# Cross-attention on one core: pairs of batches with a shared tail chunk, chunks in groups of two, and a rolled TensorE loop

## The chip, the cores and the metric

The kernel runs on one core of a Trainium2 chip. Its time is the device time of one execution in microseconds (us). Three runs of the kernel before took 1699.2, 1699.8 and 1699.86 us; the median is 1699.8 us. The engines are TensorE (PE, with its weight loads listed as PEld), VectorE (DVE), ScalarE (ACT), GpSimd (POOL) and SyncE (SP), which issues DMAs.

## What is computed

The model is one layer: cross-attention of 16 batches of 64 queries to 1601 context rows each, causal self-attention, and a mixture of experts. The change touches the cross-attention, cut here to what matters:

```python
# x (16, 64, 512), y (16, 1601, 256); 16 heads of 32; y_dca = last 16 rows, y_main = the other 1585
q  = _ln((x @ Wq + bq).reshape(b, s1, H, HD), qn_w, qn_b)          # per head
kv = concatenate([y_main @ Wk + bk, y_main @ Wv + bv], -1).reshape(b, s2, H, 2 * HD)
k  = _ln(kv[..., :HD], kn_w, kn_b);  v = kv[..., HD:]
ctx     = _attn(qT, kT, vT)                                        # softmax over 1585 keys
ctx_dca = _attn(qT, k_dcaT, v_dcaT)                                # softmax over the 16 others
x = x + (ctx + ctx_dca) @ Wo + bo
```

## The kernel before

`prepare` makes the queries, the split weights and the keys and values of the 16 other rows. `cross_attention` walks over the 16 batches, and within a batch over 13 chunks (CH = 13) of 128 context rows; the last one (LAST = 12) holds 49 rows of the main context, and beside them the 16 other rows from partition 64 on. Then come `self_attention` and `experts`.

For one chunk the work is this. ScalarE rounds the context chunk to a high part (`y_high`, L851) and GpSimd subtracts it for the low part (`y_low`, L941). TensorE multiplies by the weights of the keys (`keys`, 6 matmuls of 512 columns) and of the values (`values`, 6 more), all recorded at L96 with the tiles wk and wv. VectorE adds the bias to the keys and so empties their PSUM bank (`k_bias`, L985), GpSimd squares them (`square`, L948), VectorE reduces per head (`k_reduce`, L991), ScalarE makes a seed for the inverse root (`seed`, L102 and L104), VectorE refines and applies it (`k_norm`, L109 to L113 and L1000). ScalarE empties the values' bank (`v_evac`, L870, or L868 for the last chunk). TensorE turns the normed keys with 4 transposes (`turn`, L77 on kn) and ScalarE copies them out (`k_evac`, L858). TensorE multiplies keys by queries (`scores`, L1104: weights of 64 rows by 128 columns), ScalarE takes exponentials (`exps`, L883), and TensorE sums the values (`weighted`, L1120: weights of 128 rows by 64 columns; for the last chunk twice, once for the main context and once for the other rows).

The order on each engine is written out by hand. TensorE works in stages: for chunk c it does `keys` and `values` of chunk c + 3, `turn` of c + 2, `weighted` of c and `scores` of c + 1. The keys, the values and the turned keys have one PSUM bank each (`K_BANK`, `V_BANK`, `TR_BANK`), the scores one pair of banks, so `scores` of a chunk waits until `exps` of the chunk before has ended, `values` waits for the `v_evac` of the chunk before (semaphore ve), `keys` for its `k_bias` (kb) and `turn` for its `k_evac` (ke). Once a batch VectorE copies the next batch's queries into `qbd` (`queries`, L1008), and TensorE turns the finished context (`turn_ctx`, two transposes of ctx_sb).

`batches` has two variants of all this; a flag computed on the device picks one, and the trace shows the one without guarded scores (`Else`). In that variant TensorE's code is written out for all 16 batches one behind the other; the other engines run a loop of 15 iterations and one batch behind it.

Of the kernel before, what the change touches and what calls it, by code (L numbers as in the profile page):

```python
# [37 lines left out]
VBUFS = 4  # L38
# [84 lines left out]
LANDING = ((0, 4), (4, 8), (8, CH))  # L123


def load_context(sp, io, g, b, free=None):

    for n, (lo, hi) in enumerate(LANDING):
        end = min(hi * P, SM)
        if free:  # L130
            free(hi - 1)
        sp.dma_start(g.y[:, :, lo * P:end], io["y"][b].rearrange("(k p) t -> p k t", p=P)[:, :, lo * P:end])\
            .then_inc(g.landed[n], 16)

# [4 lines left out]
def prepare(nc, io, g, psum):  # L139
    with ExitStack() as ctx:  # L140
# [54 lines left out]
        with nc.Block() as block:  # L195
            @block.sync
            def _(sp):
# [15 lines left out]
                load_context(sp, io, g, 0)  # L213
                read_guard(sp, "sp")
# [80 lines left out]
            def _(pool):  # L295
# [9 lines left out]
                nc.gpsimd.memset(g.y_hi[:, 2].bitcast(F32), 0.0)  # L305
                nc.gpsimd.memset(g.y_lo[:, 2].bitcast(F32), 0.0)
                nc.gpsimd.memset(g.k32[:, 2], 0.0)
# [6 lines left out]
                for n in range(2):  # L314
                    nc.gpsimd.tensor_tensor(g.v_last[:, n, :, HD], g.v_last[:, n, :, HD],
                                            g.cols[:, 6 + n:7 + n].to_broadcast([P, H]), ALU.add)
# [392 lines left out]
def cross_attention(nc, io, g, psum):  # L709
    K_BANK, V_BANK, TR_BANK, S_BANK, O_BANK, CT_BANK = 0, 1, 2, 3, 5, 7  # L710

    with ExitStack() as ctx:
# [4 lines left out]
        y = g.y  # L717
# [13 lines left out]
        select = sb("select", [2, 2, P])  # L731
# [3 lines left out]
        def buf(c):  # L735

            return 2 if c == LAST else c % 2

        def at(b, c):

            return (b, c) if c < CH else (b + 1, c - CH)

        def done(b, c):


            return b * CH + (CH + c + 1)

        def before(b, c):

            return done(b, c - CH if c == LAST else c - 2 if c >= 2 else c - 3)  # L750

        def before_v(b, c):

            return done(b, c - CH if c == LAST else c - VBUFS if c >= VBUFS else c - VBUFS - 1)
# [31 lines left out]
        def ahead(c, n, room):  # L786

            return c + n < CH + room
# [8 lines left out]
        with nc.Block() as block:  # L797
            @block.sync
            def _(sp):
                def second_values(b):  # L800
                    sp.wait_ge(s["pv"], done(b, -1))
                    sp.dma_start(g.v_last[DCA_ROW:DCA_ROW + DCA, 1, :, 0:HD],
                                 io["vd"][bass.ds(b * DCA, DCA), :].rearrange("t (h n) -> t h n", h=H))\
                        .then_inc(s["vd"], 16)

                def shifts(b):
                    if not isinstance(b, int):
                        sp.wait_ge(s["qb"], b * parts(True))
                    sp.dma_start(shift_raw[:], io["shift"][b].rearrange("(s q) n -> s (q n)", s=2)).then_inc(s["shift"], 16)

# [3 lines left out]
                second_values(0)  # L814
                sp.dma_start(select[:].rearrange("s n p -> s (n p)"), io["select"]).then_inc(s["select"], 16)

                def batch(b, guarded):
                    def free(c):
                        sp.wait_ge(s["yhi"], done(b, c - CH))
                        sp.wait_ge(s["ylo"], done(b, c - CH))  # L820

                    load_context(sp, io, g, b, free)
                    if guarded:
                        shifts(b)
                    second_values(b)

                with sp.If(g.guards["sp"] != 0):
                    shifts(0)
                    with sp.Fori(1, B) as b:
                        batch(b, True)  # L830
                with sp.Else():
                    with sp.Fori(1, B) as b:
                        batch(b, False)
# [4 lines left out]
            def _(act):  # L838
                act.sem_inc(s["yhi"], CH + EARLY)
                for stage in ("ke", "ve", "ex", "klog", "kseed"):  # L840
                    act.sem_inc(s[stage], CH)
# [3 lines left out]
                def y_high(b, c):  # L845
                    b, c = at(b, c)
                    n = next(n for n, (lo, hi) in enumerate(LANDING) if lo <= c < hi)
                    w = min(P, SM - c * P)
                    act.wait_ge(g.landed[n], b * 16 + 16)
                    act.wait_ge(s["vp"], before(b, c))  # L850
                    nc.scalar.copy(g.y_hi[:, buf(c), :, 0:w], y[:, :, c * P:c * P + w]).then_inc(s["yhi"], 1)  # L851

                def k_evac(b, c):
                    b, c = at(b, c)
                    w = DCA_ROW if c == LAST else P
                    act.wait_ge(s["tr"], done(b, c))
                    act.wait_ge(s["sc"], before(b, c))
                    nc.scalar.activation(k32[:, buf(c), :, 0:w],  # L858
# [1111 lines left out]
```

## Time and profile before

| | us |
|---|---|
| median of 3 runs | 1699.8 |
| the profiled execution, its own time | 1697.8 |
| its span, first to last instruction | 1695.9 |
| cross-attention on TensorE (82.9 to 1274.6) | 1191.7 |
| of it, one batch of 13 chunks (615.66 to 689.80) | 74.14 |
| one chunk (603.13 to 608.71) | 5.58 |
| TensorE busy over the span | 1623.3 (96%) |
| VectorE, ScalarE, GpSimd busy | 811.3, 749.7, 472.1 |

The span is read from the profile's first line. The stages are found by the lines of the instructions in order of time; the durations of single steps are differences of start times, since the end of a matmul is modelled and reaches into the next one. A bracket at the end of a row says how long the engine had sat idle, and what released it.

### The profile page before, as it was taken

What the parts mean: (1) busy time and instruction counts of PE and PEld (TensorE: products, weight loads), DVE (VectorE), ACT (ScalarE), POOL (GpSimd) and SP (SyncE); (2) the same over time, 40 slices, a digit from 0 to 9 for tenths busy, and PEclk for the clock granted to TensorE, in tenths of its full rate; (3) what the DMA queues carried; (4) which work ended last, traced back from release to release, by engine and by line L of the source; (5) the groups of instructions that cost most, each with busy time, mean ns of one, the idle gap of its engine ahead of it and who ended that gap; (6) DMA issues with size and microseconds to landing.
All of it is one profiled execution on the core that took longest, in us unless ns stands there. A gap on an engine that the chain in (4) does not pass through costs nothing. (4 is left out here: it accounts for less than half of the span.)

```text
span 1695.9 us, 42180 instructions
## 1 busy us (share of the span) xinstructions
PE 1623.3 (96%) x16354; PEld 1338.6 (79%) x16354; DVE 811.3 (48%) x1841; ACT 749.7 (44%) x1523; POOL 472.1 (28%) x508
## 2 busy tenths in 40 slices
PE   5699999999999999999999999999995998899999
PEld 3378888888888888888888888888874666799998
DVE  6644444445444454544444444454543555433323
ACT  2255555555555555555555555555551333311111
POOL 2233332323333232333323232332324000022012
PEclk9899999999999999999999999999997999799999
DMA  6110000000000100000000000000001000111111
GB/s 220 50 56 15 27 28 27 15 27 27 15 27 28 27 15 27 27 15 27 28 27 15 27 27 15 27 28 27 3 2 56 1 0 1 57 56 38 33 41 49
DMA packets 33736, 53.50 MB, mean 32 GB/s; under 512 B 6963, under 2 KB 13494, under 8 KB 33590
## 3 DMA queue, kind: packets, MB, share of 16 engines
q1 hardware_dynamic: 33156, 51.20, 9.7%
q8 instruction: 126, 2.06, 0.5%
q14 instruction: 20, 0.16, 0.0%
q10 hardware_dynamic: 434, 0.08, 0.0%
HBM read 48.64 MB, written 2.62 MB: 30 GB/s over the span
## 5 line engine op out<-in xcount | busy, mean ns | idle before, releaser
L941 POOL TENSOR_TENSOR y_lo<-y_sb,y_hi 128x256 fp32r<-128x256 f32 (+1 forms) x206 | 146.7, 712 | 686.2 <-ACT y_hi L851 686.2
L883 ACT ACTIVATE probs<-psum 128x1024 f32<-128x1024 f32 x208 | 213.5, 1027 | 172.5 <-PE psum L1104 172.2
L991 DVE TENSOR_REDUCE kss<-ksq 128x16 f32<-128x512 f32 x208 | 142.7, 686 | 241.4 <-POOL ksq L948 241.4
L870 ACT COPY v_sb<-psum 128x512 f32<-128x512 f32 x192 | 112.7, 587 | 313.3 <-PE psum L96 313.2
L948 POOL TENSOR_TENSOR ksq<-kc 128x512 f32<-128x512 f32 x208 | 216.4, 1041 | 92.0 <-DVE kc L985 89.3
L1104 PE MATMUL psum<-qbd,k 64*128 64x128 f32 x3328 | 241.7, 285 | 0.0
L985 DVE TENSOR_TENSOR kc<-psum,bk_sb 128x512 f32<-128x512 f32 x208 | 143.7, 691 | 199.7 <-PE psum L96 199.7
L1120 PEld LDWEIGHTS psum<-v_sb,probs 128*64 128x64 f32 x6144 | 194.7, 138 | 33.4 <-issue 31.9
L1120 PE MATMUL psum<-v_sb,probs 128*64 128x33 f32 x6144 | 216.1, 224 | 1.1 <-ACT probs L883 1.1
L1104 PEld LDWEIGHTS psum<-qbd,k 64*128 64x128 f32 x3328 | 201.9, 187 | 8.9 <-issue 0.2
L96 PE MATMUL psum<-wk_hi,y_hi 128*128 128x512 f32 x416 | 187.2, 450 | 8.8 <-issue 8.7
L96 PE MATMUL psum<-wv_hi,y_hi 128*128 128x512 f32 x416 | 165.3, 397 | 0.0
L96 PE MATMUL psum<-wk_hi,y_lo 128*128 128x512 f32 x416 | 164.9, 396 | 0.0
L96 PE MATMUL psum<-wk_lo,y_hi 128*128 128x512 f32 x416 | 164.4, 395 | 0.0
L96 PE MATMUL psum<-wv_hi,y_lo 128*128 128x512 f32 x416 | 164.3, 395 | 0.0
L96 PE MATMUL psum<-wv_lo,y_hi 128*128 128x512 f32 x416 | 163.6, 393 | 0.0
L858 ACT ACTIVATE k<-psum,cols_sb 128x512 f32<-128x512 f32 (+1 forms) x208 | 159.6, 767 | 5.2 <-PE psum L77 5.2
L1000 DVE SCALAR_TENSOR_TENSOR kn<-kc,kr 128x512 f32<-128x512 f32 x208 | 149.0, 717 | 8.7 <-DVE kr L113 0.3
L77 PEld LDWEIGHTS psum<-ident_sb,kn 128*128 128x128 f32 x832 | 101.8, 140 | 37.6 <-DVE kn L1000 12.1
L77 PE MATMUL psum<-ident_sb,kn 128*128 128x128 f32 x832 | 125.7, 274 | 4.5 <-DVE kn L1000 4.5
L96 PEld LDWEIGHTS psum<-wk_hi,y_hi 128*128 128x128 f32 x416 | 78.0, 187 | 44.0 <-issue 9.2
L1660 POOL TENSOR_TENSOR wg_lo<-expert_raw,wg_hi 128x1536 fp32r<-128x1536 f32 x4 | 14.0, 3490 | 308.4 <-DVE wg_hi L1758 308.4
(221 smaller groups left out, 2279.9 us busy)
## 6 DMA issues: line engine op xcount, KB each, us to landing
y_sb<-in_y SPq DMA_DIRECT2D x32, 512.0 KB, 3.5
y_sb<-in_y SPq DMA_DIRECT2D x16, 561.0 KB, 3.7
expert_raw<-in_wg SPq DMA_DIRECT2D x5, 768.0 KB, 4.7
expert_raw<-in_wu SPq DMA_DIRECT2D x5, 768.0 KB, 4.6
expert_raw<-in_wd SPq DMA_DIRECT2D x5, 768.0 KB, 4.5
out_dram<-x_sb SPq DMA_DIRECT2D x8, 256.0 KB, 2.0
x_sb<-in_x SPq DMA_DIRECT2D x1, 1536.0 KB, 9.6
wq<-in_wq SPq DMA_DIRECT2D x4, 256.0 KB, 4.4
```

The costliest lines, as they stand in the source:

```text
L77: last = pe.transpose(bank[:, k * P:(k + 1) * P], src[:, k * P:(k + 1) * P], ident)
L96: last = pe.matmul(bank, lhs, rhs, start=(n == 0), stop=(n == len(todo) - 1))
L858: nc.scalar.activation(k32[:, buf(c), :, 0:w], psum[:, TR_BANK, :].rearrange("p (g t) -> p g t", g=GROUPS)[:, :, 0:w], ACT.Identity, scale ...
L870: nc.scalar.copy(g.v[:, c % VBUFS, :, 0:HD], bank).then_inc(s["ve"], 1)
L883: nc.scalar.activation(probs[:, buf(c), :], psum[:, S_BANK:S_BANK + 2, :].rearrange("p a n -> p (a n)"), ACT.Exp, scale=SCALE).then_inc(s[ ...
L941: nc.gpsimd.tensor_tensor(g.y_lo[:, buf(c), :, 0:w], y[:, :, c * P:c * P + w], g.y_hi[:, buf(c), :, 0:w].bitcast(F32), ALU.subtract).then_ ...
L948: nc.gpsimd.tensor_tensor(sq[:, buf(c)], kc[:, buf(c)], kc[:, buf(c)], ALU.mult).then_inc(s["ksq"], 1)
L985: nc.vector.tensor_tensor(kc[:, buf(c)], psum[:, K_BANK, :], g.bk[:], ALU.add).then_inc(s["kb"], 1)
L991: nc.vector.tensor_reduce(ss[:, buf(c)], head_view(sq[:, buf(c)]), AX_X, ALU.add).then_inc(s["krd"], 1)
L1000: nc.vector.scalar_tensor_tensor(out=head_view(kn[:, buf(c)]), in0=head_view(kc[:, buf(c)]), scalar=HD ** 0.5, in1=spread(kr[:, buf(c)], H ...
L1104: last = pe.matmul(out[n][a], k32[rows, buf(c), n, :], g.qbd[rows, n, :], start=not guarded, stop=True, skip_group_check=True)
L1120: last = pe.matmul(psum[j * SQ:(j + 1) * SQ, O_BANK + n, p * VW1:(p + 1) * VW1], probs[:, buf(c), place(h) * SQ:(place(h) + 1) * SQ], v, s ...
```

## The change

Batches are taken in pairs (i = 0 to 7). The 49 last rows of both batches of a pair come as one chunk: batch 2i on partitions 0 to 48, batch 2i + 1 on 64 to 112 (`y_tail`, prepared on the host, loaded by its own DMA, `load_tails`). So a pair has 25 projected chunks (PROJ) and still 26 units of attention (UNITS). For the shared chunk `k_evac` and `v_evac` copy in two pieces, into separate buffers for the two batches.

The 26 units are taken in 12 groups: five of two, and one of three that holds the tail, for each batch. For group n TensorE does `keys` and `values` of the chunks of group n + 2 alternating with `turn` of those of group n + 1, then `weighted` of all units of group n, then `scores` of all units of group n + 1. The scores now have two pairs of banks, used alternately; the values have 6 buffers instead of 4. The banks for that are found by putting the second sum of a tail into V_BANK (so its `weighted` waits for the latest `v_evac`, and the next `values` for `o_evac`) and the turned context into TR_BANK (so `turn` waits for `ctx_evac`). `o_evac` is two copies instead of one. The other engines' orders follow the groups.

TensorE's code is no longer written out: every engine runs a loop of 7 iterations, one for a pair, with a prefetch hint for the closing branch at the top of each iteration, and one pair behind it.

```diff
+VBUFS = 6
+TAIL, PROJ, UNITS = LAST, 2 * CH - 1, 2 * CH
+GROUP = [[u + CH * half for u in ((2 * n, 2 * n + 1) if n < 5 else (10, 11, 12))] for half in range(2) for n in range(6)]
+GR = len(GROUP)
...
             def run(guarded):
                 first(guarded)
-                if name == "pe" and not guarded:
-                    for b in range(B - 1):
-                        steps(b, CH, guarded)
-                else:
-                    with eng.Fori(0, B - 1) as b:
-                        steps(b, CH, guarded)
-                steps(B - 1, 0, guarded)
+                with nc.Fori(0, B // 2 - 1, engines=[eng.engine], hint_back_edge=True) as i:
+                    steps(i, GR, guarded)
+                steps(B // 2 - 1, 0, guarded)
...
+                    if tail(n):
+                        for half, first in enumerate(TAIL_ROWS):
+                            act.wait_ge(s["sc"], unit(i, same_tail((TAIL, UNITS - 1)[half])))
+                            last = nc.scalar.activation(k32[:, 2 + half, :, first:first + LM], bank[:, :, first:first + LM],
+                                                        ACT.Identity, scale=g.cols[:, 2:3], bias=g.cols[:, 3:4])
...
+                def steps(i, room, guarded):
+                    for group in range(GR):
+                        for j, u in enumerate(units(group, room)):
+                            exps(i, u, j)
+                        if group in (1, 7):
+                            ctx_evac(i * 2 + group // 6)
+                        project, turned, high = (projections(group + n, room) for n in (2, 1, 3))
+                        for j in range(3):
+                            if j < len(project):
+                                v_evac(i, project[j])
+                            if j < len(turned):
+                                k_evac(i, turned[j])
+                            if j < len(high):
+                                y_high(i, high[j])
+                            if j < len(project):
+                                seed(i, project[j])
+                        if group in (5, 11):
+                            o_evac(i * 2 + group // 6, i, GROUP[group][-1])
...
+                def chunks(i, ns):
+                    for j, n in enumerate(ns):
+                        k_bias(i, n)
+                        if j:
+                            k_norm(i, ns[j - 1])
+                        k_reduce(i, n)
+                    if ns:
+                        k_norm(i, ns[-1])
...
+                    pe.wait_ge(s["ex"], unit(i, u - 1 if column(u) == 0 else u - 3 if column(u) == 1 else u - 2))
...
-                    for c in range(CH):
-                        if ahead(c, 3, room):
-                            keys(b, c + 3)
-                            values(b, c + 3)
-                        if ahead(c, 2, room):
-                            turn(b, c + 2)
-                        if c == 2:
-                            turn_ctx(b)
-                        weighted(b, c)
-                        if ahead(c, 1, room):
-                            scores(b, c + 1, guarded)
+                    latest = PROJ - 1
+                    for group in range(GR):
+                        project, turned = projections(group + 2, room), projections(group + 1, room)
+                        if group in (1, 7):
+                            pe.wait_ge(s["ke"], projected(i, turned[0] - 1))
+                            turn_ctx(i * 2 + group // 6)
+                        for j in range(3):
+                            if j < len(project):
+                                keys(i, project[j])
+                                if j == 0 and group in (0, 6):
+                                    pe.wait_ge(s["oe"], i * 2 + (group // 6 + 1))
+                                values(i, project[j])
+                                latest = project[j]
+                            if j < len(turned):
+                                if j == 0 and group in (1, 7):
+                                    pe.wait_ge(s["ce"], i * 2 + (group // 6 + 2))
+                                turn(i, turned[j])
+                        for u in units(group, room):
+                            weighted(i, u, latest)
+                        for j, u in enumerate(units(group + 1, room)):
+                            scores(i, u, j, guarded)
```

On TensorE, one stage of the steady part before, from the end of `values` on (kn: `turn`, v_sb: `weighted`, qbd: `scores`, wk_hi: the next `keys`):

```order
L96 MATMUL psum<-wv_hi,y_lo 128x512
L77 MATMUL psum<-ident_sb,kn 128x128 x4
L1120 MATMUL psum<-v_sb,probs 64x33 x16
L1104 MATMUL psum<-qbd,k 128x128 x8
L96 MATMUL psum<-wk_hi,y_hi 128x512
```

The same place in the kernel after, at the end of a group of two:

```order
L100 MATMUL psum<-wv_hi,y_lo 128x512
L81 MATMUL psum<-ident_sb,kn 128x128 x4
L1211 REGISTER_ALU
L1222 MATMUL psum<-v_sb,probs 64x33 x16
L1211 REGISTER_ALU
L1222 MATMUL psum<-v_sb,probs 64x33 x16
L1205 MATMUL psum<-qbd,k 128x128 x16
L1163 REGISTER_ALU
L100 MATMUL psum<-wk_hi,y_hi 128x512
```

Two `weighted` and two `scores` now stand together, and the other `turn` of the group stands between `values` and `keys`.

On TensorE in the group before a tail (group 4 of a pair, which turns the chunks 10, 11 and 12), the kernel after has two `turn` in a row, the second of which waits for the `k_evac` of the first (xa_ke):

```order
L100 MATMUL psum<-wv_hi,y_lo 128x512
L81 MATMUL psum<-ident_sb,kn 128x128 [waits xa_ke,xa_km]
L81 MATMUL psum<-ident_sb,kn 128x128 x3
L81 MATMUL psum<-ident_sb,kn 128x128 [waits xa_ke,xa_km]
L81 MATMUL psum<-ident_sb,kn 128x128 x3
L1211 REGISTER_ALU
L1222 MATMUL psum<-v_sb,probs 64x33 [waits xa_ve,xa_ex]
L1222 MATMUL psum<-v_sb,probs 64x33 x15
```

Before, a `turn` was followed by `weighted` everywhere:

```order
L96 MATMUL psum<-wv_hi,y_lo 128x512
L77 MATMUL psum<-ident_sb,kn 128x128 [waits xa_ke,xa_km]
L77 MATMUL psum<-ident_sb,kn 128x128 x3
L1120 MATMUL psum<-v_sb,probs 64x33 [waits xa_ve,xa_ex]
L1120 MATMUL psum<-v_sb,probs 64x33 x15
```

On ScalarE in the same group, the kernel after has the second chunk's `v_evac`, `k_evac`, `y_high` and `seed`, then the two pieces of the tail's `k_evac`, then the three `exps`:

```order
L942 REGISTER_ALU
L950 COPY v_sb<-psum 128x16x32
L936 ACTIVATE k<-psum,cols_sb 128x512
L923 CAST y_hi<-y_sb 128x256
L106 ACTIVATE klog<-kss,cols_sb 128x16
L108 ACTIVATE kseed<-klog 128x16
L932 ACTIVATE k<-psum,cols_sb 128x4x49 x2
L961 REGISTER_ALU
L964 ACTIVATE probs<-psum 128x1024
```

Before, ScalarE had one of each per chunk, with `exps` at its head:

```order
L883 ACTIVATE probs<-psum 128x1024
L851 CAST y_hi<-y_sb 128x256
L865 REGISTER_ALU
L870 COPY v_sb<-psum 128x16x32
L858 ACTIVATE k<-psum,cols_sb 128x512
L102 ACTIVATE klog<-kss,cols_sb 128x16
L104 ACTIVATE kseed<-klog 128x16
```

So the `k_evac` on which the second of two adjoining `turn` waits stands behind a `v_evac` that waits for `values`.

## Rows read from the trace of the kernel before

**Rows 1.** The page: busy time and share of the span by engine.

```profile
PE 1623.3 (96%) x16354; PEld 1338.6 (79%) x16354; DVE 811.3 (48%) x1841; ACT 749.7 (44%) x1523; POOL 472.1 (28%) x508
```

**Rows 2.** Busy by stretch, one batch, two later ones: PE, PEld, DVE, ACT, POOL, PEclk.

```profile
615.66:689.80 74.14, 73.92 (x869) 61.61 (x867) 36.20 (x85) 40.02 (x80) 24.74 (x29) 1.00 0.08 24
1275.00:1306.00 31.00, 14.71 (x38) 7.85 (x39) 15.77 (x20) 4.42 (x12) 17.11 (x10) 0.67 0.26 77
1459.00:1483.00 24.00, 23.66 (x107) 23.39 (x108) 11.94 (x46) 10.35 (x18) 0.00 (x0) 0.51 0.27 97
```

**Rows 3.** Timeline of one steady chunk, TensorE: start, length, line, count.

```profile
603.13 0.50 PE L96 MATMUL psum<-wk_hi,y_hi 128*128 128x512 f32 x1
603.47 0.40 PE L96 MATMUL psum<-wk_lo,y_hi 128*128 128x512 f32 x1
...
605.80 0.39 PE L96 MATMUL psum<-wv_hi,y_lo 128*128 128x512 f32 x1
606.03 0.60 PE L77 MATMUL psum<-ident_sb,kn 128*128 128x128 f32 x4
606.56 1.13 PE L1120 MATMUL psum<-v_sb,probs 128*64 128x33 f32 x32
607.62 1.16 PE L1104 MATMUL psum<-qbd,k 64*128 64x128 f32 x16
608.71 0.50 PE L96 MATMUL psum<-wk_hi,y_hi 128*128 128x512 f32 x1
```

**Rows 4.** Timeline of TensorE: inside a run of scores, of transposes; the tail's sum.

```profile
602.81 0.39 PE L1104 MATMUL psum<-qbd,k 64*128 64x128 f32 x4
602.92 0.28 PE L1104 MATMUL psum<-qbd,k 64*128 64x128 f32 x2
...
612.58 2.06 PE L1120 MATMUL psum<-v_last,probs 128*64 128x33 f32 x64
614.57 1.16 PE L1104 MATMUL psum<-qbd,k 64*128 64x128 f32 x16
...
629.73 0.60 PE L77 MATMUL psum<-ident_sb,kn 128*128 128x128 f32 x4
630.16 0.38 PE L77 MATMUL psum<-ident_sb,ctx_sb 128*128 128x128 f32 x2
```

**Rows 5.** Timeline in the experts: transposes, then matmuls with 128x128 weights.

```profile
1489.58 0.49 PE L77 MATMUL psum<-ident_sb,moe_h 128*128 128x128 f32 x3
...
1490.09 0.34 PE L96 MATMUL psum<-wg_lo,moe_xhi 128*128 128x384 f32 x1
1490.26 0.34 PE L96 MATMUL psum<-wg_hi,moe_xlo 128*128 128x384 f32 x1
```

**Rows 6.** Timeline of TensorE at a batch's end: last value product, turn.

```profile
611.38 0.40 PE L96 MATMUL psum<-wv_hi,y_lo 128*128 128x512 f32 x1
612.00 0.66 PE L77 MATMUL psum<-ident_sb,kn 128*128 128x128 f32 x4 [0.22 <-DVE kn L1000]
```

**Rows 7.** Timeline of the steady chunk, ScalarE.

```profile
606.31 0.59 ACT L870 COPY v_sb<-psum 128x512 f32<-128x512 f32 x1 [1.74 <-PE psum L96]
606.79 0.79 ACT L858 ACTIVATE k<-psum,cols_sb 128x512 f32<-128x512 f32 x1
608.83 1.03 ACT L883 ACTIVATE probs<-psum 128x1024 f32<-128x1024 f32 x1 [0.78 <-PE psum L1104]
```

**Rows 8.** Branches (ns min/median/max, first and last start), and a matmul behind one.

```profile
L770 PEldq COMPARE_BRANCH  x1: 4144/4144/4144, 78.6 to 78.6; - x1
...
L1844 PEldq COMPARE_BRANCH  x2: 76/146/215, 1584.2 to 1690.0; - x2
...
1586.93 0.33 PE L96 MATMUL psum<-wg_hi,moe_xhi 128*128 128x384 f32 x1
```

**Rows 9.** DMA queue of TensorE's code in 155:1214: packets, MB, share.

```profile
q8 instruction: 100, 1.64, 0.6%
```

**Rows 10.** Timeline of TensorE behind the last values of the last batch.

```profile
1269.26 1.13 PE L1120 MATMUL psum<-v_sb,probs 128*64 128x33 f32 x32 [1.12 <-ACT probs L883]
```

More of the change, by code:

```diff
@@ L784, in place, with projections, units @@
             return (h // 2 % 2) * 8 + h // 4 * 2 + h % 2
-        def ahead(c, n, room):
-            return c + n < CH + room
+        def projections(group, room):
+            if group >= GR + room:
+                return []
+            turn, group = group // GR, group % GR
+            return [turn * PROJ + u for u in GROUP[group] if u < PROJ]
+        def units(group, room):
+            if group >= GR + room:
+                return []
+            turn, group = group // GR, group % GR
+            return [turn * UNITS + u for u in GROUP[group]]
         def normalise(b, wait, engine):
@@ L853, in k_evac @@
[L853 to L858, printed above, removed]
-                                         psum[:, TR_BANK, :].rearrange("p (g t) -> p g t", g=GROUPS)[:, :, 0:w],
-                                         ACT.Identity, scale=g.cols[:, 2:3], bias=g.cols[:, 3:4]).then_inc(s["ke"], 1)
@@ new lines, in v_evac @@
+                def v_evac(i, n):
+                    i, n = at(i, n, PROJ)
+                    bank = psum[:, V_BANK, :].rearrange("p (h n) -> p h n", h=H)
+                    act.wait_ge(s["vp"], projected(i, n))
+                    if tail(n):
+                        for half in range(2):
+                            rows = slice(half * 64, half * 64 + 64)
+                            act.wait_ge(s["pv"], unit(i, same_tail((TAIL, UNITS - 1)[half])))
+                            last = nc.scalar.copy(g.v_last[rows, half, 0, :, 0:HD], bank[rows])
+                    else:
+                        act.wait_ge(s["pv"], unit(i, v_user(n)))
+                        last = nc.scalar.copy(g.v[:, (n - n // CH) % VBUFS, :, 0:HD], bank)
+                    last.then_inc(s["ve"], 1)
@@ L993, in k_norm @@
[L993 to L1001 removed]
+                    dve.sem_inc(s[stage], PROJ)
@@ L1047, in steps @@
+                def steps(i, room, guarded):
+                    for group in range(1, GR + 1 if room else GR):
+                        if group in (5, 11) and (group == 5 or room):
+                            queries(i * 2 + (1 if group == 5 else 2), i, TAIL if group == 5 else UNITS - 1, guarded)
+                        if group in (6, 12):
+                            dve.wait_ge(s["oe"], i * 2 + (group // 6 + 1))
                             nc.vector.reciprocal(rinv[:], o_sb[:, :, :, HD]).then_inc(s["rc"], 1)
+                        chunks(i, projections(group + 2, room))
+                        if group in (1, 2):
+                            second_keys(i, group - 1)
@@ L1059, in _ @@
             def _(pe):
[L1060 to L1067 removed]
+                for stage in ("kp", "vp", "tr"):
+                    pe.sem_inc(s[stage], PROJ)
+                for stage in ("sc", "pv"):
+                    pe.sem_inc(s[stage], UNITS)
```

465 lines of the change are left out of this document (246 added, 219 removed).

## The prediction, made before the run

> **What bounds the kernel now.** I read the page's busy times first [rows 1]: TensorE is busy 1623.3 of 1695.9 us, 96%, and no other engine reaches half. So only what shortens TensorE's own row of work, or makes it wait, can move the time. The stretches say where it lies [rows 2]: one batch takes 74.14 us, TensorE is busy for 73.92 of them at a granted clock of 1.00, VectorE for 36.2, ScalarE for 40.0, GpSimd for 24.7. Sixteen such batches are about 70% of the span. Then I read one chunk in order of time [rows 3]: keys begin at 603.13 and again at 608.71, 5.58 us later, with no bracket of idle time between. Every chunk of a batch repeats this, but for the tail and one `turn`. What a chunk is made of: twelve projections, from second to last start 605.80 - 603.47 = 2.33 us for ten steps, 0.233 each, 2.80 in all; four transposes 0.43 (629.73 to 630.16); sixteen head sums 0.93 (the tail's 32 take 614.57 - 612.58 = 1.99, an ordinary chunk's 16 take 1.06 from 606.56 to 607.62, the difference is the second 16); eight score products 0.89, a pair of rows each 0.11 us apart (602.81, 602.92) [rows 3, 4]. These add up to 5.05. The other 0.53 us is busy time too by the page, and it lies at the borders: the first key product takes 0.34 instead of 0.233, transposes take 0.53 ahead of the sums instead of 0.43, the sums 1.06 instead of 0.93, the scores 1.09 (607.62 to 608.71) instead of 0.89. Values to transposes costs nothing (605.80 to 606.03 is 0.23). The borders that cost are those at which the weights' shape changes: 128x128, 128x64, 64x128 in the rows' own words.
>
> [...]
>
> **What the change takes away.** (a) One projected chunk of 26 in each pair: 2.80 + 0.43 = 3.23 us, eight times, 25.8 us. Its scores and sums stay: the units are still 26 in a pair. (b) Borders. Before, each of 26 units pays 0.53. Now a group pays one each of scores to keys, transposes to sums, sums to scores, and there are 12 groups: 14 borders fewer in each pair, 112 in all, 59.4 us. New is transposes to keys inside a group, both 128x128. The experts have this border [rows 5]: from the first of 3 transposes to the second matmul 0.51 us, where 3 x 0.11 + 0.17 = 0.50 is owed. I take nothing; the upper bound is a border's price of 0.1 to 0.2 us, 104 times, 10 to 20 us, but that would need a change of shape. (c) The wait at a batch's end. VectorE copies the next batch's queries, its `k_norm` comes late, and `turn` starts 0.62 instead of 0.23 us behind the last value product (611.38 to 612.00) [rows 6]. Its `turn` is now a group (over 10 us) behind its `k_norm`, so 15 x 0.39 = 5.9 us go. Sum: 91.1 us.
>
> **What it adds.** I laid the group out by the rows' durations, keys at 0: second product at 0.34, first values 1.50 to 2.89, `turn` to 3.33, second keys to 4.72, second values to 6.12, `turn` to 6.55, sums from 6.65, scores from 8.6, next group at 10.6 us. The tightest hand-off inside it: the second values need the first `v_evac`. That starts 0.51 us behind the start of the last value product and takes 0.59 (605.80, 606.31) [rows 3, 7], so it ends at about 3.76 and is wanted at 4.72; 0.96 us to spare. The key bank stands about as well. All else (norm chain, exponentials, splits) has two or more us. (d) Group 4 has two adjoining `turn`. The second needs the first's `k_evac`, which sits on ScalarE behind the second `v_evac` (the last value product starts at 5.89, the `v_evac` 0.51 later at 6.40, the next operation 0.48 after it, then 0.79 us [rows 7]) and ends at 7.66; the `turn` could have begun at 6.55. 1.15 us, once a pair: 9.2 us. Queued behind it on TensorE are that group's sums and scores, so all of it is paid. Bounds: 0 to 1.5 each. (e) The third scores of a group of three need the bank whose `exps` is the first unit's: it starts 1.21 behind its scores and takes 1.03 (607.62, 608.83) [rows 3, 7], ready at 2.30; the third scores are due after 2 x 0.89 + 0.10 = 1.89. 0.41 us, 16 times, 6.6 us. (f) The waits on a register's value need an extra instruction each on TensorE's sequencer; it runs ahead of the array (it had taken the experts' back edge at 1584.2, while that iteration's first matmul began at 1586.93 [rows 8]), so nothing. (g) The closing branch, 6 times taken (7 iterations). At L770 TensorE jumps over code that is not at hand, and the branch takes 4.14 us; the experts' loop, by its code 576 matmuls and as many weight loads an iteration, closes in 0.22 us, and the next iteration begins without a bracket of idle time [rows 8]. The new body is two batches of 869 + 867 instructions less one chunk's 32, about 3440; the code queue moves 16 KB blocks, 100 of them in 14.3 batches [rows 9], 7 a batch, so a body is 13 to 14 blocks. It is three times as long as the experts' body, and I take it that its head is gone when the branch comes. The hint is there to fetch it. No row shows a hinted branch: between 0.22 us, hidden by the lead, and 4.14 each. I take 0, because TensorE's stream of code is sequential otherwise and the hint stands a whole iteration ahead; 0 to 25 us go into the range. ScalarE's and VectorE's bodies double as well; a stall there of 4 us would cost TensorE about 1, since the first `v_evac` of a pair is wanted only at 4.7 us.
>
> (h) The ends. The last batch's waits, up to 1.12 us [rows 10] and some 3 us together, come from working one unit at a time; with groups of two and three about half of them stay, and the start has one small wait fewer: 1.5 us gained, 0 to 3. (i) The loads: the tail's DMA is small and its consumer a group or more away; the DMA share is 0.08 [rows 2]. Nothing. The two small copies in place of one `o_evac`, and of the tail's `k_evac`, lie in ScalarE's idle time, more than 30 of 74 us.
>
> **Sum.** 1697.8 - 91.1 + 9.2 + 6.6 - 1.5 = 1621.0 us. That is against the profiled execution, which was 2.0 us below the median of 1699.8; so I forecast **1623 us**, 4.5% less. One thing beside the sum: the granted clock is at half speed for parts of two later stretches (0.67 of 31 us, 0.51 of 24 us) [rows 2], around the joints to self-attention and to the experts. Everything behind the cross-attention now starts some 77 us earlier, and these stretches may fall 10 us longer or shorter, 5 us either way.
>
> **The rivals.**
> 1. *The branch is not covered.* Then each of 6 back edges shows what is left of L770's 4.14 us after the sequencer's lead of up to 2.7: 1.4 to 4.1 each, 9 to 25 us, about 1640 us. For it: 3440 instructions are not at hand after a jump back of 13 blocks. Against: the hint. [...]
> 2. *A hand-off inside the group is late.* Banks for keys and values are single, and 0.96 us is all there is. If ScalarE's queue or contention on VectorE uses it up and 0.5 us more, 96 groups give 48 us back: 1671 us. For it: the layout rests on one chunk's durations. Against: the layout above, with every step ahead of it done.
> 3. *The borders are not what costs 0.53.* If it is each unit's waits and not its shapes, only (a), (c) and (h) remain against (d) and (e): 1697.8 - 25.8 - 5.9 - 1.5 + 15.8, about 1680, 1682 with the median. Against: keys to values also begins with waits and costs nothing.
> 4. *Slower than before.* After a jump back the fetching of code no longer runs ahead, and each of 7 x 13.5 = 94 blocks shows on TensorE. It decides from 77 / 94 = 0.8 us a block on; at 4.14 less 1 us of lead it is 295 us, 1918 us. Against: behind the experts' back edge the matmuls begin without idle time [rows 8], and before the change a body of code seven blocks long is fetched in every batch with none to be seen [rows 2, 9].
> 5. *Better.* (d) and (e) don't appear and the ends give more: 1606 us.
>
> **How the numbers follow.** The forecast has 0.64 (its own range 1613 to 1633, from (d), (e), (h) and the clock), rival 1 0.13, rival 2 0.08, rival 3 0.04, rival 4 0.03, rival 5 0.08. From 1606 to 1645 us lie the forecast, rival 5's middle and rival 1: about 0.8. A difference of 0.2%, 3.4 us, is about what can be told from none. All but rival 4 and a far end of rival 2 are faster by more: faster 0.95, same 0.01, slower 0.04.
>
> **What the profile after would show.** Groups of about 10.6 us on TensorE, keys to keys of the same place; sums in blocks of 64 rows and scores of 32; `keys` right behind `turn` with no gap; 400 projections of each kind instead of 416. A gap of about 1.15 us ahead of one `turn` a pair, put down to `k_evac`, and 0.4 ahead of a third scores, put down to `exps`. A pair takes about 139 us instead of 148.3. No gap where the loop closes, and a branch row of well under 1 us; 3 or 4 us there is rival 1. A wait of `values` on v_sb or of `keys` on kc in every group is rival 2. The forecast is wrong if the pair is not within 137 to 141 us.

## The result, and the profile after

The changed kernel takes **1622.6 us** (median of 4 runs, 1621.8 to 1623.2) against 1699.6 us (1699.2 to 1699.9) for the kernel before: a ratio of 0.955, with a 95% interval of 0.954 to 0.956. The forecast was 1623 us. The profiled execution took 1622.7 us with a span of 1620.8, 75.1 us less than before.

First the page's busy times, which answer to [rows 1].

```profile
PE 1539.8 (95%) x16226; PEld 1302.3 (80%) x16226; DVE 848.0 (52%) x1793; ACT 739.9 (46%) x1515; POOL 463.5 (29%) x492
```

TensorE is still what bounds the kernel: its busy time fell by 83.5 us, its share hardly moved, and nothing else comes near. The stretches that answer to [rows 2], with the same columns (length; busy time and count of PE, PEld, DVE, ACT, POOL; granted clock; DMA share; GB/s), are one group of two, one pair, and a short stretch at the start at half clock.

```profile
401.57:412.16 10.59, 10.59 (x131) 9.12 (x129) 6.22 (x13) 6.36 (x14) 4.27 (x5) 1.00 0.07 11
378.83:517.36 138.53, 136.79 (x1722) 118.06 (x1720) 76.82 (x163) 78.82 (x159) 48.18 (x56) 1.00 0.09 26
97.90:101.30 3.40, 3.40 (x11) 2.49 (x9) 3.30 (x7) 1.14 (x4) 1.27 (x2) 0.51 0.02 5
```

A group is 10.59 us where 10.6 was forecast, a pair 138.5 where about 139 was forecast and two batches took 148.28 before. The next rows are the timeline of TensorE in that group, which answers to [rows 3].

```profile
401.57 0.50 PE L100 MATMUL psum<-wk_hi,y_hi 128*128 128x512 f32 x1
...
404.24 0.39 PE L100 MATMUL psum<-wv_hi,y_lo 128*128 128x512 f32 x1
404.47 0.60 PE L81 MATMUL psum<-ident_sb,kn 128*128 128x128 f32 x4
404.82 0.47 PE L100 MATMUL psum<-wk_hi,y_hi 128*128 128x512 f32 x1
405.13 0.39 PE L100 MATMUL psum<-wk_lo,y_hi 128*128 128x512 f32 x1
...
406.29 0.39 PE L100 MATMUL psum<-wv_hi,y_hi 128*128 128x512 f32 x1
...
407.65 0.60 PE L81 MATMUL psum<-ident_sb,kn 128*128 128x128 f32 x4
408.18 2.06 PE L1222 MATMUL psum<-v_sb,probs 128*64 128x33 f32 x64
410.17 2.06 PE L1205 MATMUL psum<-qbd,k 64*128 64x128 f32 x32
412.16 0.50 PE L100 MATMUL psum<-wk_hi,y_hi 128*128 128x512 f32 x1
```

Read it start to start. Two sums take 1.99 us together and two scores 1.99, where single ones took 1.06 and 1.09. The second keys follow `turn` after 0.35 us, and the product behind them comes 0.31 us later; before it was 0.43 for a run of four transposes and 0.23 for a step. Together that is within 0.02 us of nothing: transposes to keys has no price.

The whole stage, from its first key product to the last value sum, went from 1191.76 us (82.90 to 1274.66) to 1114.80 us (82.64 to 1197.44), 76.96 us less; the sum's terms give 76.8. What follows it took 421.3 us before and 423.4 after; it runs the same work on TensorE, and what differs most are the stretches at half clock, 44.4 us together before and 51.2 after. The stage also begins 0.26 us earlier, which together makes the 75.1 us of the span.

The two added waits stand in group 4.

```profile
431.57 0.60 PE L81 MATMUL psum<-ident_sb,kn 128*128 128x128 f32 x4
433.18 0.63 PE L81 MATMUL psum<-ident_sb,kn 128*128 128x128 f32 x4 [1.01 <-DVE kn L1098]
433.74 2.06 PE L1222 MATMUL psum<-v_sb,probs 128*64 128x33 f32 x64
435.73 2.06 PE L1205 MATMUL psum<-qbd,k 64*128 64x128 f32 x32
438.01 1.16 PE L1205 MATMUL psum<-qbd,k 64*128 64x128 f32 x16 [0.23 <-ACT probs L964]
```

The same place on ScalarE and VectorE tells what `turn` really waits for.

```profile
424.97 0.69 DVE L1098 SCALAR_TENSOR_TENSOR kn<-kc,kr 128x512 f32<-128x512 f32 x1
...
431.77 0.58 ACT L950 COPY v_sb<-psum 128x512 f32<-128x512 f32 x1 [1.17 <-PE psum L100]
432.25 0.78 ACT L936 ACTIVATE k<-psum,cols_sb 128x512 f32<-128x512 f32 x1
```

The second `turn` starts 1.61 us behind the first instead of 0.43: 1.18 us, forecast 1.15. The bracket names VectorE's `kn`, since a `kn` ends at 433.18; but by VectorE's order that one belongs to the first chunk of group 6, and the norm that this `turn` needs, of chunk 12, had ended at 425.66 (the row at 424.97). The `turn` starts 0.15 us behind the end of `k_evac` (432.25 + 0.78 = 433.03), the bank's other user; in experiment 9, where `k_evac` comes earlier, it follows 0.14 us behind it too. The third scores come 2.28 us behind the first instead of 1.89: 0.39 us, forecast 0.41.

The closing branch, with the columns of [rows 8], and the place where the pair closes at 380 us:

```profile
L802 PEldq COMPARE_BRANCH  x7: 87/796/966, 240.5 to 1070.6; - x7
```

```profile
377.93 2.06 PE L1205 MATMUL psum<-qbd,k 64*128 64x128 f32 x32
380.25 0.49 PE L100 MATMUL psum<-wk_hi,y_hi 128*128 128x512 f32 x1 [0.27 <-issue]
```

It takes 0.8 us on TensorE's sequencer (0.97 here), but begins at 378.8, 1.1 us before the array is due to take the next keys (377.93 + 1.99 = 379.92), so little of it shows: scores to keys take 2.32 us here instead of the 1.99 of an ordinary group. Over the six edges the extra is 0.20, 0.34, 0.17, 0, 0.32 and 0, about 1.0 us in all.

### The profile page after: what moved, and what is told of

The parts are those of the page before. It is cut to its first block and busy times, and to the rows that moved or that the text cites. A ratio compares the mean times of both kernels' runs of the same rounds, so it can differ in the third digit from the quotient of the medians.

```text
span 1620.8 us, 42323 instructions
## 1 busy us (share of the span) xinstructions
PE 1539.8 (95%) x16226; PEld 1302.3 (80%) x16226; DVE 848.0 (52%) x1793; ACT 739.9 (46%) x1515; POOL 463.5 (29%) x492
## 5 line engine op out<-in xcount | busy, mean ns | idle before, releaser
L1038 POOL TENSOR_TENSOR ksq<-kc 128x512 f32<-128x512 f32 x200 | 208.1, 1041 | 445.6 <-DVE kc L1083 443.7
L964 ACT ACTIVATE probs<-psum 128x1024 f32<-128x1024 f32 x208 | 202.7, 1022 | 87.8 <-PE psum L1205 87.6
L1205 PE MATMUL psum<-qbd,k 64*128 64x128 f32 x3328 | 216.0, 279 | 3.8 <-ACT probs L964 3.2
L1031 POOL TENSOR_TENSOR y_lo<-y_sb,y_hi 128x256 fp32r<-128x256 f32 x190 | 139.1, 732 | 226.5 <-ACT y_hi L923 226.5
L1222 PEld LDWEIGHTS psum<-v_sb,probs 128*64 128x64 f32 x6144 | 186.9, 138 | 17.6 <-issue 17.5
L1222 PE MATMUL psum<-v_sb,probs 128*64 128x33 f32 x6144 | 197.6, 224 | 0.0
L100 PE MATMUL psum<-wk_hi,y_hi 128*128 128x512 f32 x400 | 176.8, 442 | 10.8 <-issue 8.5
L936 ACT ACTIVATE k<-psum,cols_sb 128x512 f32<-128x512 f32 x192 | 150.6, 785 | 1.3 <-PE psum L81 0.8
L1098 DVE SCALAR_TENSOR_TENSOR kn<-kc,kr 128x512 f32<-128x512 f32 x200 | 141.4, 707 | 7.3 <-DVE kr L117 0.4
L115 DVE SCALAR_TENSOR_TENSOR ktmp<-ktmp,kseed 128x16 f32<-128x16 f32 x200 | 116.5, 583 | 6.8
```

What stands on the lines that cost most here:

```text
L100: last = pe.matmul(bank, lhs, rhs, start=(n == 0), stop=(n == len(todo) - 1))
L115: nc.vector.scalar_tensor_tensor(out=tmp, in0=tmp, scalar=-0.5, in1=seed, op0=ALU.mult, op1=ALU.mult).then_inc(second, 1)
L936: last = nc.scalar.activation(k32[:, buf(n)], bank, ACT.Identity, scale=g.cols[:, 2:3], bias=g.cols[:, 3:4])
L964: nc.scalar.activation(probs[:, buf(u), :], psum[:, bank:bank + 2, :].rearrange("p a n -> p (a n)"), ACT.Exp, scale=SCALE).then_inc(s["ex" ...
L1031: nc.gpsimd.tensor_tensor(g.y_lo[:, buf(n)], src, g.y_hi[:, buf(n)].bitcast(F32), ALU.subtract).then_inc(s["ylo"], 1)
L1038: nc.gpsimd.tensor_tensor(sq[:, buf(n)], kc[:, buf(n)], kc[:, buf(n)], ALU.mult).then_inc(s["ksq"], 1)
```

## The experiments

Nine kernels ran. Theory: the gain is the removed chunk and the removed changes of weight shape; the added costs are the two waits of group 4 and of the groups of three; a hint on the branch covers the fetching of code. Each run comes with the kernel before on the same chip.

### 1. Sums and scores alternate inside a group

```diff
-for u in units(group, room):
-    weighted(i, u, latest)
-for j, u in enumerate(units(group + 1, room)):
-    scores(i, u, j, guarded)
+for j in range(3):
+    if j < len(summed):
+        weighted(i, summed[j], latest)
+    if j < len(scored):
+        scores(i, scored[j], j, guarded)
```

> The kernel after, but TensorE alternates weighted and scores inside a group (sum, scores, sum, scores) instead of two sums and then two scores. No work, buffer or wait is added. Theory (the borders between weight shapes cost): each of the 96 groups gets one more sums-to-scores border (0.20 us) and one more scores-to-sums border (0.13 us), 32 us; the third scores of a group of three is then a sum later behind the first and no longer waits 0.4 us for its exponentials, 16 times, minus 6 us: about 1648 us. Rival (each unit's waits cost the 0.53 us, not the shapes): no change, 1616 to 1623 us.

Measured: **1647.5 us**, ratio 0.969 (0.968 to 0.971). It is 24.9 us above the changed kernel, as expected. TensorE's timeline in this kernel, a group with two sums and three scores:

```profile
441.26 1.13 PE L1222 MATMUL psum<-v_sb,probs 128*64 128x33 f32 x32
442.32 1.16 PE L1205 MATMUL psum<-qbd,k 64*128 64x128 f32 x16
443.41 1.12 PE L1222 MATMUL psum<-v_sb,probs 128*64 128x33 f32 x32
444.47 2.06 PE L1205 MATMUL psum<-qbd,k 64*128 64x128 f32 x32
```

Every change between the two kinds brings the old durations back (1.06 and 1.09), with no bracket of idle time in these rows, while the number of products is the same; the third scores no longer wait. Inside a run of two sums or two scores the second unit's waits are still there and cost nothing. So the 0.53 us of a unit lie at the changes and not at its waits. Rival 3 falls. The run multiplies sums to scores and brings in scores to sums; that transposes to sums and scores to keys cost by shape as well is read from the rows, and which side of the shape matters was not varied.

### 2. No hint on the closing branches

```diff
-with nc.Fori(0, B // 2 - 1, engines=[eng.engine], hint_back_edge=True) as i:
+with nc.Fori(0, B // 2 - 1, engines=[eng.engine]) as i:
```

> The kernel after without the prefetch hints, on all engines. Theory (the hint is what fetches the loop's head): each of TensorE's 6 taken back edges takes 3.4 to 4.1 us as the jump at the variants does, some 1 us of it hidden by the sequencer's lead, so 2.4 to 3.1 us of gap each, 14 to 19 us less the 1 us of gaps that the hinted edges show: 1636 to 1641 us; the other engines' back edges stay at 0.05 us. Rival (the blocks come in time anyhow): back edges under 1 us and 1622.6 us.

Measured: **1651.2 us**, ratio 0.971 (0.970 to 0.973), 28.5 us above the changed kernel, 4.8 for each of the six edges taken. The branch's row, and the keys behind the first edge:

```profile
L802 PEldq COMPARE_BRANCH  x7: 83/3597/3887, 240.8 to 1102.4; - x7
```

```profile
244.73 0.79 PE L100 MATMUL psum<-wk_hi,y_hi 128*128 128x512 f32 x1 [2.73 <-issue]
245.32 0.63 PE L100 MATMUL psum<-wk_lo,y_hi 128*128 128x512 f32 x1
```

The branch takes 3.6 us, most of it shown on TensorE as 2.7. The expectation had that and missed two things that come behind. First, the granted clock is at half (0.50 in 244.3:247.7) for 3.4 us from 244.3 (steps of 0.43 us instead of 0.23), and so at each of the six edges, once for 6.8 us; from the first keys to the first `turn` that costs 1.4 us. Second, VectorE stops at its own edge. Its branch row is 0.06 us long, but its next instruction comes 4 us later, and the keys behind it on TensorE wait:

```profile
260.00 0.69 DVE L1083 TENSOR_TENSOR kc<-psum,bk_sb 128x512 f32<-128x512 f32 x1 [3.72 <-issue]
260.84 0.47 PE L100 MATMUL psum<-wk_hi,y_hi 128*128 128x512 f32 x1 [0.56 <-DVE kc L1083]
```

These keys start 1.16 us behind their `turn` instead of 0.35: 0.8 us here, 0.7 to 1.1 at the other edges. VectorE has this stop of 3.6 to 4.0 us at all six edges; in the changed kernel and the other runs with its hint the next instruction comes after 0.2 us. The hints of all engines together are worth 28 us here; the theory is right in kind and was 10 to 15 us too low.

### 3. TensorE's pairs written out

```diff
+if name == "pe" and not guarded:
+    for i in range(B // 2 - 1):
+        steps(i, GR, guarded)
+else:
     with nc.Fori(0, B // 2 - 1, engines=[eng.engine], hint_back_edge=True) as i:
         steps(i, GR, guarded)
```

> The kernel after with TensorE's unguarded pairs written out one behind the other again, as the kernel before had its batches; the other engines keep their loops. Theory (the rolled loop costs only what shows at its back edges): the six gaps of 0 to 0.34 us, 1.0 us together, go: 1621.6 us. Rival (waits on register values cost TensorE at every group): more than 5 us less, under 1618 us.

Measured: **1621.4 us**, ratio 0.954 (0.953 to 0.955), 1.2 us below the changed kernel, and the runs of the two overlap (1620.9 to 1622.4 against 1621.8 to 1623.2). In its trace no border between scores and keys is longer than 0.25 us, where the looped kernel has four of 0.37 to 0.54. Read from the borders, the hinted loop costs 1 us of 1622; the times alone can't tell it.

### 4. `turn` first in group 4

In group 4 alone TensorE takes `turn` ahead of `keys` and `values`, and ScalarE `k_evac` ahead of `v_evac`.

```diff
 for j in range(3):
+    if group == 4 and j < len(turned):
+        turn(i, turned[j])
     if j < len(project):
         keys(i, project[j])
...
-    if j < len(turned):
+    if group != 4 and j < len(turned):
```

> The kernel after, but in the group before a batch's shared tail (group 4) TensorE does each turn ahead of the keys instead of behind the values, and ScalarE its k_evac ahead of the v_evac, so that no two turns adjoin. Theory (the second of two adjoining turns waits 1.18 us for the k_evac behind the v_evac, and all of it is paid): 8 x 1.18 = 9.4 us less, 1613 us, and no gap in front of a turn. Rival (the wait only moves: the moved turns find the keys' norm late, or the scores behind them wait): 1618 to 1623 us.

Measured: **1611.2 us**, ratio 0.948 (0.947 to 0.950), 11.4 us below the changed kernel. The stage takes 1104.4 us instead of 1114.8. Of these 10.4 us, 9.4 are the eight waits of 1.18; about 1 is the half clock of 97.9 to 101.3, which did not come in this kernel. What follows the stage took 2.2 us less as well; its stretches at half clock were 41.0 us instead of 51.2. Term (d) of the sum is confirmed with its size, and it can be had back.

### 5 and 6. The kernel before, TensorE in a loop over one batch, with and without a hint

```diff
-if name == "pe" and not guarded:
-    for b in range(B - 1):
-        steps(b, CH, guarded)
-else:
-    with eng.Fori(0, B - 1) as b:
-        steps(b, CH, guarded)
+with nc.Fori(0, B - 1, engines=[eng.engine], hint_back_edge=(name == "pe")) as b:
+    steps(b, CH, guarded)
```

The second kernel has `eng.Fori(0, B - 1)` instead, with no hint.

> The kernel before, with TensorE in a loop over one batch (15 iterations, 14 back edges) whose closing branch is hinted; nothing else differs. Theory (a hinted edge shows 0 to 0.34 us on TensorE, as in the changed kernel): 0 to 5 us longer than before, 1700 to 1704 us. Rival (the kernel before also gained from being written out, and the loop itself costs more than the edges show): over 1708 us.

> As the one before, but without the hint. It asks how much of a body stays at hand: a batch's code is 7 blocks, half a pair's 13 to 14. Theory (a batch's code is not kept either, each of 14 back edges shows about the 4.8 us that an unhinted edge cost in the changed kernel): 1699.5 + 14 x 4.8 = 1767 us, with 1740 as the lower end (2.7 us each, without the half-speed clock behind it). Rival (the code of one batch stays at hand as the experts' does): 1700 to 1704 us, the same as hinted.

Measured: **1698.3 us** with the hint, ratio 1.000 (0.999 to 1.001), and **1809.2 us** without, ratio 1.065 (1.063 to 1.067). The queue of TensorE's code in 155:1214 had 100 blocks in the kernel before [rows 9]. Here are the hinted loop's queue and its branch:

```profile
q8 instruction: 2, 0.03, 0.0%
```

```profile
L762 PEldq COMPARE_BRANCH  x15: 80/216/258, 170.9 to 1208.7; - x15
```

And the unhinted loop's queue, its branch, and TensorE behind the edge at 500 us:

```profile
q8 instruction: 116, 1.90, 0.7%
```

```profile
L762 PEldq COMPARE_BRANCH  x15: 79/3322/3784, 170.7 to 1319.7; - x15
```

```profile
506.70 0.58 PE L96 MATMUL psum<-wk_hi,y_hi 128*128 128x512 f32 x1 [5.57 <-issue]
507.08 0.63 PE L96 MATMUL psum<-wk_lo,y_hi 128*128 128x512 f32 x1
```

With the hint, the batch's code of some 1820 instructions (867 products, as many weight loads, and the sequencer's own) is fetched once and then stays: two blocks in a thousand microseconds, and a branch of 0.22 us. Without it the same body is fetched anew each time, 9 blocks an iteration where the body fills 7, and each of 14 edges costs 7.9 us: at 500 us, 5.57 us in which TensorE stands still, and 6.8 us at half clock, which begin 1.9 us before it starts again (504.8 to 511.6). In that edge the code queue moves a block at 501.1 and the next only at 504.5, each in 1.0 us, so two fetches come one behind the other; what fills the time between them no view shows. My expectation for the unhinted loop (1767 us) took one fetch and was 42 us too low. Its rival, that a batch's code stays at hand without a hint, fell; but it stays with one.

A pair's body of some 3630 instructions is fetched anew even with the hint: the code queue moved 114 blocks in 155:1214 of the changed kernel. The hinted branch of experiment 5 goes back seven blocks in 0.22 us. The experts' loop of the kernel before stays at hand without a hint: its 1152 matmuls and weight loads had 4 blocks in 1484:1584, and none came in 1584:1696, behind its back edge. Why the longer body of a batch is fetched anew when nothing hints its branch, no run here shows.

### 7 and 8. The start's order, alone and with the pairs written out

On top of experiment 4, ahead of the loop: VectorE takes `k_bias` of chunk 2 ahead of the `k_norm` of chunk 1, and ScalarE `v_evac` of chunk 2 ahead of the `seed` of chunk 1.

```diff
-chunks(0, projections(0, GR))
-chunks(0, projections(1, GR))
+k_bias(0, 0)
+k_reduce(0, 0)
+k_bias(0, 1)
+k_norm(0, 0)
+k_bias(0, 2)
+k_reduce(0, 1)
+k_norm(0, 1)
...
```

> The changed kernel with turn first in group 4 (the fourth experiment), and ahead of the loop VectorE's k_bias of chunk 2 taken ahead of the k_norm of chunk 1 and ScalarE's v_evac of chunk 2 ahead of the seed of chunk 1. Theory (the start lost the forecast gain to VectorE's order): the 2.15 us wait of the keys of chunk 3 goes but for 0 to 0.3, 1611.2 - 1.9 = 1609.3 us, within 0.7. Rival (the start's loss is owed to something else, and the wait moves to the next step): 1610.8 to 1611.5 us.

> The same as e7_start_order, with TensorE's pairs written out instead of looped. Theory (six hinted edges show 1.0 to 1.2 us together): 1608.2 us. Rival (they cost nothing): the same as e7_start_order.

Measured: **1609.6 us** (1607.7 to 1610.8), ratio 0.948 (0.946 to 0.949), and **1610.2 us** (1608.2 to 1611.0), ratio 0.948 (0.946 to 0.950). The keys of chunk 3 no longer wait (in the changed kernel 2.15 us, below), and from the first keys to the first value sum it is 24.9 us instead of 26.5 in experiment 4. One wait is new, of the first group's second scores for `k_evac`:

```profile
98.57 1.16 PE L1217 MATMUL psum<-qbd,k 64*128 64x128 f32 x16
100.62 1.16 PE L1217 MATMUL psum<-qbd,k 64*128 64x128 f32 x16 [0.89 <-ACT k L936]
```

So 1.6 of the 1.9 us came, and the wait was due to the order ahead of the loop: VectorE's, by the bracket, though the run moved ScalarE's as well. That writing the pairs out gives another 1 us on top was not seen: the two kernels cannot be told apart, and only one of the looped kernel's six edges shows 0.2 us, and one 0.05. The 1.6 us itself is read from the traces; the medians' spread is as wide.

### 9. `k_evac` ahead of `v_evac` in every group

```diff
 for j in range(3):
-    if j < len(project):
-        v_evac(i, project[j])
     if j < len(turned):
         k_evac(i, turned[j])
+    if j < len(project):
+        v_evac(i, project[j])
```

> The changed kernel with ScalarE's k_evac ahead of its v_evac in every group; TensorE's order as in the changed kernel. It spends the time to spare that the forecast put at 0.96 us between the first v_evac of a group and the second values. In the changed kernel's trace v_evac starts at 404.67 and takes 0.58, and the second values are due at 406.29: about 1.0 us to spare. The k_evac can start some 0.4 us behind the last transpose, about 405.2, hands on 0.67 later, and the v_evac ends at about 406.45: 0.2 us late. Theory (the time to spare is about 1 us): 0.2 us a group on v_sb ahead of the second values, 0 to 0.5, some 88 groups, 17.6 us (0 to 44), and the wait of the adjoining turn in group 4 about 0.5 us shorter, 8 times, 4 us: 1636 us, 1626 to 1655. Rival (there is more to spare than the layout shows): no bracket at the second values, and 1618 to 1619 us for the shorter wait of turn.

Measured: **1651.9 us**, ratio 0.972 (0.971 to 0.974), 29.3 us above the changed kernel. ScalarE and TensorE in one group of it:

```profile
412.12 0.78 ACT L936 ACTIVATE k<-psum,cols_sb 128x512 f32<-128x512 f32 x1 [2.33 <-PE psum L81]
...
412.79 0.58 ACT L950 COPY v_sb<-psum 128x512 f32<-128x512 f32 x1
...
413.07 0.40 PE L100 MATMUL psum<-wk_hi,y_lo 128*128 128x512 f32 x1
...
413.51 0.47 PE L100 MATMUL psum<-wv_hi,y_hi 128*128 128x512 f32 x1
...
413.82 0.39 PE L100 MATMUL psum<-wv_lo,y_hi 128*128 128x512 f32 x1
```

The `v_evac` ends at 413.37, and the values start at 413.51 where 413.30 was due: 0.21 us late, as the layout said. Their second product then comes 0.31 us later instead of 0.23, so a stop costs 0.30. Between 120 and 1170 us 96 chunks of 184 have this wait, 88 of them of 0.21 to 0.22 us and 8 longer, none in the changed kernel; 96 times 0.30 is 29 us. That is within the range expected and above its 17.6, because the restart's 0.08 was missing and because the shorter wait of the adjoining `turn` did not come (1.56 us between the two, 1.61 in the changed kernel). The rival falls. The `v_evac` ends 4.75 us behind its group's first keys instead of 3.68: 1.07 us later, of which 0.21 show. So some 0.86 us could be spent, 0.1 less than the forecast's 0.96, which left out the 0.14 us from the end of `v_evac` to the start of the values.

The page of this kernel hardly shows the loss:

```profile
L100 PE MATMUL psum<-wv_hi,y_hi 128*128 128x512 f32 x400 | 165.4, 413 | 6.3 <-ACT v_sb L950 0.6
```

The idle column has 0.6 us put down to `v_sb` where some 29 were lost. A product's row is 0.39 us long while the next starts 0.23 behind it, so a wait of up to 0.2 us disappears under the modelled end of the one before. Only starts show it.

## Why the prediction was right, by its own steps

- **(a), (b), (c): the chunk, the borders, the wait at a batch's end (91.1 us).** Right together; their sizes were not measured one by one. A group is 10.59 us; experiment 1 shows that the 0.53 us lie at changes between products, and the rows that only changes with a new shape cost; transposes to keys is free as taken (0.35 + 0.31 us where 0.43 + 0.23 is owed). The batch-end wait is gone.
- **(d) adjoining `turn`, (e) third scores (9.2 and 6.6 us).** Right, 1.18 and 0.39 to 0.40 us apiece; experiment 4 took (d) away and got 9.4. The working was a little off: its rows give 7.66 - 6.55 = 1.11 us and not 1.15 for (d), and 1.21 + 1.03 = 2.24, so 0.35 and not 0.41, for (e), 1.3 us less in all; what the rows lack is the time from the end of one engine's work to the start of the other's, 0.15 us in group 4. The bracket, though, named `kn` and not `k_evac` as I had said it would.
- **The 0.96 us to spare ahead of the second values.** Nearly right: in the trace the first `v_evac` ends at 405.25 and the second values start at 406.29, and experiment 9 shows some 0.86 us that can be spent. Rival 2 lay as near as it looked.
- **(f) the waits on register values.** Nothing, as forecast. TensorE's sequencer has 161 ALU_OP of 32 ns each at L1163 (`keys` and `values`) and 161 at L1211 (`weighted`), and the kernel written out (experiment 3) has none at the same two waits; the whole difference of the two kernels is 1.2 us, and the edges' 1.0 is in it. Not every wait has one: at L1179 (`turn`) it is 7 beside 193 rows of waits, at L1186 (`scores`) 28 beside 176. The sequencer's lead was 2.7 us at the experts' back edge [rows 8] and is 1.1 us where a pair closes.
- **(g) the closing branch.** Taken as 0, measured 1.0 us over six edges. That the branch at L770 waited for code fits the code queue, which moved one block of 16 KB between 80 and 81 us, inside its 78.6 to 82.7. Right that a pair's body is not at hand (114 blocks in 155:1214) and that the hint covers it (28.5 us in experiment 2). The price put on the branch uncovered, 1.4 to 4.1 us each (rival 1, 1640 us), holds for the stop itself (2.5 to 3.1 us start to start). The edge as a whole costs more: experiment 2 has 4.8 each and 1651 us, since 1.4 us at half clock and 0.8 us from VectorE's own stop come with it, and the sum of that rival had neither. The second I had priced elsewhere, at about 1 us for a stop of 4; experiment 2 has 0.8 for 3.7. The 1651 us lie outside my range. Rival 4 fell: inside a pair no row of TensorE waits for its code. Rival 5's 1606 us was not reached; experiment 4, without (d), comes to 1611.
- **(h) the ends.** The one term that was wrong. I had a gain of 1.5 us, 0 to 3; by the account below the ends lost 2.4. The end gave some 1.5 (waits of 3.1 us before, 1.6 after), so the start lost some 4. This is TensorE there:

```profile
96.47 0.47 PE L100 MATMUL psum<-wk_hi,y_hi 128*128 128x512 f32 x1 [2.15 <-DVE kc L1083]
100.45 1.05 PE L81 MATMUL psum<-ident_sb,kn 128*128 128x128 f32 x4
```

and this VectorE:

```profile
95.03 0.69 DVE L1098 SCALAR_TENSOR_TENSOR kn<-kc,kr 128x512 f32<-128x512 f32 x1
95.64 0.68 DVE L1083 TENSOR_TENSOR kc<-psum,bk_sb 128x512 f32<-128x512 f32 x1
```

  The keys of chunk 3 need the bank that `k_bias` of chunk 2 empties (95.64), and VectorE's order has two `k_norm` ahead of it, the second at 95.03. That makes 2.3 us start to start. Then follow 3.4 us at half clock (0.51), in which the values and the `turn` take 1.6 us longer; experiment 4 did not have them, and its first value sum came 0.9 us earlier, since its scores then waited 0.4. I had laid out a group in steady state and not the start, where the chunks come faster than the norm chain.
- **What made up for it.** From the second pair's first keys (241.75) to the eighth's (1071.71) a pair takes 138.33 us; 14 batches of before, from 170.92 to 1208.66, take 74.12 each. The difference is 9.92 us, for eight pairs 79.4; the sum had 75.3, its 76.8 less the 1.5 of the ends. So the pairs gave 4.1 us more than forecast, although the edges' 1.0 is in them. Some 3 us of that are the groups of two, 10.59 us where the chunks of before give 2 x 5.58 - 0.53 = 10.63. The stage gained 76.96, so the ends lost 2.4, which is 3.9 off. The agreement of 76.96 with 76.8 is partly luck: an error of 3.9 us at the ends against one of 4.1 in the pairs.
- **The clock behind the stage.** 6.8 us more at half clock than before and 2.1 us more time, inside the 5 us allowed.

The best version run is experiment 7, 1609.6 us, 5.3% below the kernel before.

## What to carry to other kernels

TensorE was busy 96% of the time, and yet the times between its starts held 0.53 us a unit more than its products cost inside a run. That sat at changes of the weights' shape, and putting equal shapes next to each other bought it back: alternating them again cost 24.9 us (experiment 1). The single banks' hand-offs set how far this could go: some 0.86 us to spare, and 29.3 us lost where it was overdrawn (experiment 9). So that slack is worth laying out row by row, the start included. For a loop with a body as long as those here (a batch's or a pair's) hint the closing branch: without it an edge cost 7.9 us (experiment 6) and 4.8 (experiment 2), the stretch at half clock behind it counted in. Read short waits from starts, not from the idle column, which had 0.6 us of those 29; and check by index whether the instruction in the bracket is the one that was waited for: ahead of the second `turn` it belonged to another chunk, and the bank's other user, 0.15 us before, was the cause. A short branch row doesn't show that an edge is free (VectorE's 0.06 us had a stop of 3.6 to 4.0 behind it in experiment 2): look at the next instruction of every engine in the loop.

## What was not expected of the hardware

- A hint does more than fetch the target in time: a body of some 1820 instructions stays at hand with it (2 blocks fetched in 1059 us) and is fetched anew without it (116 blocks), 1698.3 against 1809.2 us.
- At the unhinted edge of experiment 2 TensorE stood still for 2.7 us (3.1 at most), and 3.4 us at a granted clock of 0.50 began as it started again; with 5.6 us in experiment 6 it was 6.8 us, at 0.50 too. It is not a matter of the stop alone: the stop of 2.15 us at the start was followed by such a stretch in the changed kernel and by none in experiment 4.
- The closing branches of ScalarE and VectorE took 40 to 85 ns with the hint and without. ScalarE went on behind it in 0.16 us, but VectorE stood still for 3.6 to 4.0 us where its body was a pair's (experiment 2), and not where it was a batch's (experiment 6, where its next instruction came 0.21 us behind the branch). In experiment 2 a second code queue moved 68 blocks in 155:1214, in the changed kernel 10.
- A stop of 0.21 us ahead of the values cost 0.30 (experiment 9): at the restart the second product comes 0.31 instead of 0.23 us behind the first.
